# A mixture-of-experts layer on one core: experts in units of 256 tokens instead of 128, and the first layer as three fp32r products instead of one fp32 product

## The reference, cut to what matters

```python
gates = jnp.max(router_probs, axis=-1, keepdims=True)
idx = jnp.argmax(router_probs, axis=-1)                 # one of 8 experts for each token
xn = (xt - mu) * jax.lax.rsqrt(var + LN_EPS) * ln_g + ln_b
h = jnp.einsum('te,td,edf->tf', onehot, xn, W1) + b1[idx]   # W1: 8 x 256 x 1024
h = jax.nn.relu(h)
y = jnp.einsum('te,tf,efd->td', onehot, h, W2) + b2[idx]    # W2: 8 x 1024 x 256
x = x + jnp.tanh(g_ffn[0]) * (y * gates)
```

## Time and profile before

| | |
|---|---|
| Median of 3 runs | 326.51 us (326.13 to 327.85) |
| The profiled execution's own span | 325.8 us |
| PE busy | 285.8 us, 88% of the span |
| DVE, ACT, POOL busy | 211.3, 180.7, 134.3 us |
| First-layer products (L1552) | 672 records, 83.8 us busy |
| Second-layer products (L1573) | 480 records, 62.7 us busy |
| Indirect gathers (L365), scatters (L371) | 23 and 20 |

### The profile page before, as it was taken

One profiled execution on the slowest core, in us unless ns is written; L12 is line 12 of the kernel. 1 busy time (PEld: TensorE's weight loads), 2 busy tenths in 40 slices (PEclk: granted clock), 3 DMA queues, 4 the chain that ended last, 5 costly groups with the idle time before them and its releaser, 6 DMA issues.

```text
span 325.8 us, 7783 instructions
## 1 busy us (share of the span) xinstructions
PE 285.8 (88%) x2476; PEld 264.3 (81%) x2476; DVE 211.3 (65%) x666; ACT 180.7 (55%) x485; POOL 134.3 (41%) x247
## 2 busy tenths in 40 slices
PE   6769999988899999988456999999999999999980
PEld 3549788877788888877226999999999999999980
DVE  4478788999898888778772774345446644334650
ACT  2324677677676666654325875544458744455550
POOL 2434345444455555332535167322234842333241
PEclk9797999999999999999765999999999999999995
DMA  6999990000004445441123102222111121121200
GB/s 153 296 294 374 382 358 18 33 36 35 34 35 161 164 161 167 166 157 68 65 66 100 34 13 61 68 60 70 56 49 56 41 85 50 51 69 51 69 29 4
DMA packets 19890, 34.52 MB, mean 106 GB/s; under 512 B 2564, under 2 KB 14656, under 8 KB 19845
## 3 DMA queue, kind: packets, MB, share of 16 engines
q1 hardware_dynamic: 15509, 21.29, 20.1%
q0 software_dynamic: 4192, 12.62, 12.2%
q10 hardware_dynamic: 144, 0.07, 0.1%
HBM read 27.61 MB, written 6.88 MB: 106 GB/s over the span
## 4 chain that ended last, share of the span: by engine, by line
PE 61%; DVE 11%; ACT 9%; issue 7%; DMA 3%; POOL 3%; POOLq 1%; SPq 1%; DVEq 0%; ACTq 0%
PE pS L1552 22%; PE pB L1573 15%; PE pB L1350 6%; PE pA L1257 4%; PE pT L1257 4%; PE pS L1306 3%; PE pB L1375 3%; DVE mx L799 2%; DVE Pb L807 2%; DMA cst<-in_consts_dram 2%; ACT QT L512 2%; DMA zin<-rows_dram,idxg 1%; ACT PT L526 1%; PE pA L1285 1%; ACT Pb L518 1%
## 5 line engine op out<-in xcount | busy, mean ns | idle before, releaser
L1552 PE MATMUL pS<-znf,W1c 128*128 128x128 f32 x672 | 83.8, 279 | 0.0
L1552 PEld LDWEIGHTS pS<-znf,W1c 128*128 128x128 f32 x672 | 80.7, 197 | 0.0
L1573 PE MATMUL pB<-W2p,hT 128*128 128x256 f32 x480 | 62.7, 286 | 0.3 <-POOL W2p L377 0.2
L1573 PEld LDWEIGHTS pB<-W2p,hT 128*128 128x128 f32 x480 | 58.7, 191 | 0.9 <-POOL W2p L377 0.7
L1181 DVE TENSOR_SCALAR hA<-pS,b1s 128x128 f32<-128x128 f32 x84 | 23.6, 345 | 54.6 <-PE pS L1552 54.6
L371 POOL DMA_INDIRECT out_dram<-yo,idxs x20 | 21.5, 1075 | 72.7 <-DVE yo L1195 54.9
L683 ACT ACTIVATE hA<-pS,b1s 128x128 f32<-128x128 f32 x84 | 23.9, 367 | 44.4 <-PE pS L1552 44.4
L1350 PE MATMUL pB<-VB,PT 128*128 128x51 f32 (+1 forms) x320 | 37.3, 272 | 0.0
L1350 PEld LDWEIGHTS pB<-VB,PT 128*128 128x128 f32 (+1 forms) x320 | 37.0, 192 | 0.0
L518 ACT ACTIVATE Pb<-Pb 128x616 f32<-128x616 f32 x32 | 23.2, 724 | 22.8 <-DVE Pb L807 22.8
L694 ACT ACTIVATE hT<-hA 128x512 fp32r<-128x512 f32 x42 | 27.1, 645 | 8.0 <-DVE hA L1181 7.9
(11 more groups left out here) (198 smaller groups left out, 491.8 us busy)
## 6 DMA issues: line engine op xcount, KB each, us to landing
W1s<-in_L_ffn_W_dram SPq DMA_DIRECT2D x8, 1024.0 KB, 10.4
W2s<-in_L_ffn_W_dram SPq DMA_DIRECT2D x8, 1024.0 KB, 11.3
rows_dram<-pay POOLq DMA_DIRECT2D x16, 260.0 KB, 2.6
xs<-in_x_dram SPq DMA_DIRECT2D x3, 512.0 KB, 7.8
W2s<-in_sel_dram SPq DMA_DIRECT2D x1, 385.0 KB
zin<-rows_dram,idxg POOLq DMA_INDIRECT x23, 3.4
out_dram<-yo,idxs POOLq DMA_INDIRECT x20
W1s<-in_L_xattn_wk_dram SPq DMA_DIRECT2D x1, 256.0 KB, 3.0
```

The lines of the kernel that those rows point to most:

```text
L1552: t = e.matmul(pS[:, 2 * (s % 2) + n, 128 * c:128 * c + 128], W1c[k][n][:, 128 * c:128 * c + 128], znf[s % 2][:, 128 * k:128 * k + 128], s ...
L1573: t = e.matmul(o, hT[s % 2][a][:, 128 * c:128 * c + 128], W2p[b_][c // 2][:, D * (c % 2):D * (c % 2) + D], start=False, stop=(c == 7 and a ...
```

## The change

The expert stage walks over units of 256 tokens of one expert. Counts are rounded up to 256 (`ROUND2`), `NU` = 15 units and `NS` = 30 half units are the most that can occur, 8 units are always run. The one-hot matrices of the sorting get `NK` = 32 columns where there were 24. A new array `slot_two` says whether a unit's second half holds any token; PE loads it for each unit and branches on it, and runs `output` for one half or for two. Gather and scatter stay at 128 tokens, two a unit, the second half's always too. The gather of a buffer still waits until its last user is written out; the six buffers now are three units.

The first layer works like the second: W1 and z are split in two parts, and `hidden` is 48 products of 256 columns a unit. `hT`, `zf`, `zr` and `W1p` have one buffer each, and the hidden values pass through a ring of three (`hA`). The core of the diff:

```diff
             def gather(s):
                 if s >= NZ:
                     e.wait_ge(g["dve_y"], s - NZ + 1)
-                    e.wait_ge(g["pe_zT"], s - NZ + 1)
+                    e.wait_ge(g["pe_zT"], (s - NZ) // 2 + 1)
...
+            def unit(u):                                # POOL
+                if u:
...
+                        W2_low(u, 2, r_e)
+                        W2_low(u, 3, r_e)
...
+                if u + 2 < NU:
+                    regs(u + 2)
+                    W1_lows(u + 2)
+                for s in (2 * u + NZ, 2 * u + NZ + 1):
+                    if s < NS:
+                        gather(s)
+                scatter(2 * u)
+                scatter(2 * u + 1)
...
+            def layer_in(u):                            # ACT
+                e.wait_ge(g["pe_zT"], u + 1)
+                if u:
+                    e.wait_ge(g["dve_zl"], u)
                 for k in range(2):
+                    e.activation(zf[:, k, :], pA[:, 256 * k:256 * k + 256], ACT.Identity, scale=lgc[:, k:k + 1],
+                                 bias=lbc[:, k:k + 1]).then_inc(g["act_zf"], 1)
+                e.wait_ge(g["act_zf"], 2 * u + 2)
+                e.activation(zr[0][:, :, :], zf[:, :, :], ACT.Copy).then_inc(g["act_zh"], 1)
...
+            def high(u, n):
+                q = 4 * u + n
...
+                if u:
+                    e.wait_ge(g["pe_y"], q - 3)
+                e.activation(hT[0][n][:, :], hA[q % NA][:, :], ACT.Copy).then_inc(g["act_hT"], 1)
...
+            W1_high(0, 0)
+            W1_high(0, 1)
+            layer_in(0)
...
+            for n in range(4):
+                W2_high(0, n)
+            relu(0, 0)
+            relu(0, 2)
             layer_in(1)
+            W1_highs(1)
+            for n in range(4):
+                high(0, n)
...
+            def unit(u):                                # ACT
...
+                            W2_high(u, n)
...
+                if u + 1 < NU:
+                    relu(u + 1, 0)
+                    relu(u + 1, 2)
+                if u + 2 < NU:
+                    regs(u + 2)
+                    layer_in(u + 2)
+                    W1_highs(u + 2)
+                if u + 1 < NU:
+                    for n in range(4):
+                        high(u + 1, n)
...
+            def W1_low(u, k):                           # DVE; two more on POOL
+                e.wait_ge(g["act_W1h"], 4 * u + k + 1)
+                e.tensor_tensor(W1p[1][k][0][:, :], W1s[:, bass.ds(r_of[u][0] * 2048 + 1024 * k, 512)],
+                                W1p[0][k][0][:, :], ALU.subtract).then_inc(g["dve_W1l"], 1)
...
+            def z_low(u):
+                e.wait_ge(g["act_zh"], u + 1)
+                e.tensor_tensor(zr[1][:, :, :], zf[:, :, :], zr[0][:, :, :], ALU.subtract).then_inc(g["dve_zl"], 1)
...
+            def unit(u):                                # DVE
...
+                        W2_low(u, 0)
+                        W2_low(u, 1)
...
+                    relu(u + 1, 1)
+                if u + 2 < NU:
+                    regs(u + 2)
+                    z_low(u + 2)
+                    W1_lows(u + 2)
+                if u + 1 < NU:
+                    low(u + 1, 0)
+                    relu(u + 1, 3)
+                    low(u + 1, 1)
+                    low(u + 1, 2)
+                out_rows_of(2 * u)
+                out_rows_of(2 * u + 1)
+                if u + 1 < NU:
+                    low(u + 1, 3)
...
+            def hidden(u):                              # PE
+                e.wait_ge(g["act_zh"], u + 1)
+                for n in range(4):
+                    if n == 0:
+                        e.wait_ge(g["act_W1h"], 4 * u + 2)
+                        e.wait_ge(g["dve_W1l"], 2 * u + 2)
+                        e.wait_ge(g["dve_zl"], u + 1)
+                    elif n == 2:
+                        e.wait_ge(g["act_W1h"], 4 * u + 4)
+                        e.wait_ge(g["pool_W1l"], 2 * u + 2)
...
+                    for c in range(2):
+                        lo = 256 * (n % 2) + 128 * c
+                        for k in range(2):
+                            for a, b_ in ((0, 0), (0, 1), (1, 0)):
+                                t = e.matmul(pS[:, n, 256 * c:256 * c + 256], W1p[a][k][n // 2][:, lo:lo + 128],
+                                             zr[b_][:, k, :], start=(k == 0 and (a, b_) == (0, 0)),
+                                             stop=(k == 1 and a == 1))
...
             transpose_z(0)
+            hidden(0)
             transpose_z(1)
...
+            def unit(u):                                # PE
+                if u + 1 < NU:
+                    hidden(u + 1)
+                if u + 2 < NU:
+                    transpose_z(u + 2)
+                two = e.value_load(slot_two[0:1, u:u + 1], min_val=0, max_val=1)
+                with e.If(two > 0):
+                    output(u, 2)
+                with e.Else():
+                    output(u, 1)
```

More of the change, by code:

```diff
@@ L452, in slot, with W1_lows @@
-            def slot(s):
-                if s:
-                    r_e, new = r_new[s]
+            regs(0)
+            for x_ in range(E):
+                e.wait_ge(d_W1[x_], 16)
+            for k in range(2):
+                W1_low(0, k, r_new[0][0])
+            for x_ in range(E):
+                e.wait_ge(d_W2[x_], 16)
+            for n in (2, 3):
+                W2_low(0, n, r_new[0][0])
+            for s in range(4, NZ):
+                gather(s)
+            regs(1)
+            def W1_lows(u):
+                r_e, new = r_new[u]
+                with e.If(new > 0):
+                    W1_low(u, 0, r_e)
+                    W1_low(u, 1, r_e)
+                with e.Else():
+                    e.memset(ticks[2][:, u:u + 1], 0.0).then_inc(g["pool_W1l"], 2)
@@ L486, in _ @@
-            from_slot(NT)
+            for u in range(T // 256):
+                unit(u)
+            from_unit(T // 256)
         @block.scalar
@@ new lines, in W1_high, with W1_highs @@
+            def W1_high(u, n):
+                if u:
+                    e.wait_ge(g["pe_h"], 4 * (u - 1) + 2 * n + 2)
+                for k in range(2):
+                    e.activation(W1p[0][k][n][:, :], W1s[:, bass.ds(r_of[u][0] * 2048 + 1024 * k + 512 * n, 512)],
+                                 ACT.Copy).then_inc(g["act_W1h"], 1)
+            def W1_highs(u):
+                with e.If(r_of[u][1] > 0):
+                    W1_high(u, 0)
+                    W1_high(u, 1)
+                with e.Else():
+                    e.activation(ticks[0][0:1, u:u + 1], cst[0:1, 0:1], ACT.Copy).then_inc(g["act_W1h"], 4)
@@ L762, in _, with from_unit @@
+            def from_unit(u):
+                with e.If(used > u):
+                    unit(u)
+                    if u + 1 < NU:
+                        from_unit(u + 1)
+            for u in range(T // 256):
+                unit(u)
+            from_unit(T // 256)
         @block.vector
```

450 lines of the change are left out of this document (186 added, 264 removed).

## The result

The changed kernel takes 368.69 us, the median of four runs (367.49 to 370.15), where the kernel before took 326.51 beside it: ratio 1.124, 95% interval 1.116 to 1.131 (ratios are estimated from the single runs and are not the quotient of two medians). The forecast was 368 us. The profiled execution is the one of 370.15 us; its span is 368.3 us against 325.8, 42.5 us more.

A forecast was written before the change was run, and what follows sets the result against it. The prediction took the stage as bound by what PE has to issue; its terms summed to 41.3 us on a span of 325.8, 367.1, and with 0.7 for the median of runs 368 us, range 346 to 382.

The forecast's parts named there:

- PE's own work: On TensorE: 624 first-layer products at 0.120 us save 0.3 us; extra transposes and bias products cost more: +1.4 us.
- sorting and start: Before the first product: wider sorting matrices, +0.3 us, and waiting for both halves of unit 0, +2.8 us.
- unit 1, idle: Before unit 1's first layer: PE idles while its layer input and expert 1's W1 parts are made, +4.1 us.
- the clock at the start: After the gap before unit 1: TensorE's clock falls to its lower level, +2.3 us.
- unit 2: At unit 2, with a new expert: output(0) gives only 3.1 us of cover for 4.1, +1.0 us.
- gathers (2.2 + 3.4 + 3.3 + 4.1): Transposes wait for landings: ordinary units 2.2, behind units 1 and 6 3.4, behind 4, 5, 9 3.3, unit 0 4.1 us.
- register load: Behind the second half's transposes: PE loads slot_two only after the gather wait, +0.9 us at transposes 3 to 13, +9.9.
- the clock inside: At unit 0's late gather: the clock may fall again, +1.0 us (0 to 2.3).
- tail: At the end: late rows of unit 11, two unused gathers and another scatter before the last scatter, +5.5 us.
- first rival: Expert stage: gathers land in time and the slot_two load is hidden, 17.4 us are left, 344 us; chance 0.12.
- DVE's order: On DVE: output rows stand behind z's low part, low parts and relu; next gather 1.7 or 1.1 us late.
- third rival: Expert stage: the clock falls at transposes 4, 7, 8, 9 and 12, 5 x 2.3 us more, 379 us; chance 0.12.

The follow-up runs named there:

- by the run: PE loads slot_two at the start of the unit, ahead of hidden, against the changed kernel: 365.17 us, ratio 1.106.
- the layer that nobody uses: Against the kernel with three edits and filling products, the last used unit issues no first layer, transposes, weight parts and gathers for an unused one: 338.90 us.
- the longer fp32 layer: Against the changed kernel, the first layer is again one fp32 product, but of 256 columns, units kept: 371.94 us, ratio 1.129.

## Why the prediction was right

The total held, and the picture with it: PE's work nearly unchanged, hand-overs onto its path. That it held to within 1 us is in part luck, for single terms were off by up to 4 us and cancelled. Term by term, in the order of the sum, against the trace and the runs:

| term | said | shown |
|---|---|---|
| PE's own work | 1.4 | 13 x 5.70 = 74.1 us against 75.2 for the first layer, the rest as said: 0.6 |
| sorting and start | 3.1 | 4.5, of which 2.1 lie ahead of the changed code: 2.4 |
| unit 1, idle | 4.1 | 3.9 |
| the clock at the start | 2.3 | 7.23 - 5.86 in unit 1, and 0.2 more in unit 0 than before: 1.6 |
| unit 2 | 1.0 | 0.8 |
| gathers (2.2 + 3.4 + 3.3 + 4.1) | 13.0 | 14.1, of which 11.7 are counted as idle |
| register load | 9.9 | 6.9, of which 4.0 are counted as idle; 5.9 of it gone by the run |
| the clock inside | 1.0 | three falls: 2.2 + 1.5 + 1.1 = 4.8 |
| tail | 5.5 | 5.4 |

(5.86 us is what the timeline shows for 48 products at full clock, the modelled end of the last one included; the chain has 5.70 for the same. The gathers' term is the time from a first layer's start to the second half's transposes less 5.9, over eleven units. The register load's is the time from the start of the last two transposes to the bias product, 0.76 to 0.79 us in eight units and 1.02 to 1.07 in three, less 0.22, what it is where nothing waited.)

The shown ones add to 40.5 us where the sum had 41.3. The other 2.1 us of the 42.5 lie ahead of the change: the changed operation of the sorting on DVE began at 164.72 before and at 166.80 after. The attention stage, which the change doesn't touch, ran 2.1 us longer in this execution. The span of 368.3 met by 367.1 owes that much to chance.

**Right with its mechanism.** The start, from the timeline of the changed kernel:

```profile
176.41 1.02 ACT L717 ACTIVATE zf<-pA,bcol 128x256 f32<-128x256 f32 x2 [2.10 <-PE pA L1305]
177.47 0.63 ACT L720 ACTIVATE zr<-zf 128x512 fp32r<-128x512 f32 x1
178.13 0.69 DVE L1211 TENSOR_TENSOR zr<-zf,zr 128x512 fp32r<-128x512 f32 x1 [3.60 <-ACT zr L720]
178.97 8.28 PE L1614 MATMUL pS<-zr,W1p 128*128 128x256 f32 x48 [2.65 <-DVE zr L1211]
```

These are the steps of the sum one for one, 1.02, 0.63 and 0.69 us where it said 1.1, 0.63 and 0.64. Of the cases, the likeliest came true and not the rivals: the gathers didn't land in time, the load wasn't wholly hidden. The run with earlier gathers (348.0) is near what the first rival called "PE keeps its lead" (344).

**Right in the sum, not in its parts: the gathers.** From the start of a unit's first layer to the second half's transposes the sum had 6.2 us in an ordinary unit. The trace has 6.7 to 6.9 in three of them (244.93 to 251.62, 312.76 to 319.43, 342.48 to 349.34) and 5.9 and 6.0 in the two others, where PE would have been ready after 5.9: 0.5 on average and not 0.2. Its two halves were off against each other. The first gather starts 0.96 to 1.13 us after the first layer, not 1.52, for POOL answers some 0.3 us behind the rows and not 0.84. And in the three the transposes come 4.3 to 4.6 us behind the start of the second gather, where the sum had 3.4. The chain of the changed kernel splits one such time (221.24 to 225.41 above) into 3.79 us until the landing and 0.38 until PE starts, a hand-over that the sum left out. Its other landings are from 3.1 to 3.9:

```profile
261.75 3.11 DMA zin<-rows_dram,idxg
...
287.93 3.85 DMA zin<-rows_dram,idxg
```

The fit of the Trainium skill ("DMA: Bandwidth & Descriptors", Anatomy of one DMA), an estimate of 2.6 us for such a DMA, lies below each of these landings; with 2.6 the terms for the gathers would have been too small.

DVE's order does hold the gathers back as said, but by other amounts. (The steps listed for it add to 5.95 us and not 6.1, which moves nothing.) Against the ordinary 1.0 us, the first gather starts 0.3 and 1.7 us late behind the single halves 1 and 6 (said 1.7 each), 1.1, 1.7 and 1.9 behind 4, 5 and 9 (said 1.1), and 3.4 behind unit 0. Behind unit 1 it was so little because `output(1)` ran at the lower clock and gave 2.2 us more cover. What PE then waited past its 5.9 us was 0.8, 2.0, 0.9, 1.9 and 2.6 us, and 3.3 in unit 0 (said 4.1).

**Mis-sized: the register load.** I took 1.1 us from the landing to the bias product as if the load, its 0.82 us, began only behind the transposes' execution. PE's sequencer in the changed kernel, the load of `slot_two` (ns min/median/max, first and last start):

```profile
L1661 PEldq TENSOR_LOAD <-slot_two x12: 298/306/464, 197.0 to 349.3; - x12
```

It is shorter than the one of the earlier trace rows, 306 ns against 487, and the last one starts at 349.3, with the last two transposes (349.34): the sequencer loads while the array is at them. So the eleven units lose some 0.55 us in eight cases and 0.8 in three, 6.9 in all, where the sum had 0.9 us eleven times.

**Mis-sized: the clock.** I gave falls inside the stage 1.0 us, and made "the clock falls at each longer wait" a rival with 11.5 us. It fell three times: in the wait of unit 3 (211 us), at 293 and at 334. They follow the stretches from the first layer's end to the second half's transposes that took 3.3, 2.0 and 2.6 us, with the first half's two transposes inside. But a stretch of 1.9 us, at 279, had none behind it. So the third rival had the mechanism in part. These 3.8 us more and the gathers' 1.1 more stand against 3.0 less for the load and 2.6 less for PE's own work, the start, unit 1, unit 2 and the clock at the start together: the total was closer than its terms were.

## What to carry to other kernels

Where one engine bounds a pipelined loop and the rest is just hidden, a coarser step halves the number of hand-overs but also the number of steps between them: recount for each hand-over what still lies in front of it, from the buffer's release to its next use. Work that looks unused may be cover for a transfer or a preparation (the layer that nobody uses, the longer fp32 layer), so price its removal by the wait behind it, not by its own time. And a unit with a fixed price per step loses on every group that doesn't fill it: here four of twelve units paid for 256 tokens and held at most 128.

## What the runs showed of the hardware

- At full clock an fp32r product with a stationary part of 128x128 costs 0.111 us at 128 columns and 0.119 at 256; true fp32 costs 0.224 at 128 and 0.432 at 256. So fp32 went nearly with the columns between these two sizes, and fp32r hardly did: half the columns saved 7%. I had expected about 0.1 at 128 columns.
- PE stood for 4.0 us without a wait for data, once, at a branch to code behind that of all later units, and not at all with the code placed next to the branch; the branches of the earlier trace rows took 0.07 to 0.36 us. What happens in these 4.0 us no run shows.
- TensorE's clock fell to 0.50 inside the expert stage around stretches of 2.0, 2.6 and 3.3 us between two dense runs of products, with two transposes inside, and not at one of 1.9. It stayed there for some 3 to 5 us of the work that followed, which made the wait of 3.3 us cost 5.5.
- The clock can also stay low under load: with first-layer products of 128 columns it stood at 0.50 from 183 to 233 us, in which PE had one halt, of 3.9 us. Later units ran the same products at full clock.
